# Layer-1 accumulators of a graph network kernel take seven PSUM banks in turn instead of five fixed ones, and the collect of a head is issued after the second multiply of the next head, not the third

## The reference

```python
def gat_conv(x, src, dst, W, a_src, a_dst, bias, H, C, n):
    h = (x @ W).reshape(n, H, C)
    s_src = (h * a_src).sum(-1)
    s_dst = (h * a_dst).sum(-1)
    e = jax.nn.leaky_relu(s_src[src] + s_dst[dst], NEG_SLOPE)
    emax = jax.ops.segment_max(e, dst, num_segments=n)
    ee = jnp.exp(e - emax[dst])
    denom = jax.ops.segment_sum(ee, dst, num_segments=n)
    alpha = ee / denom[dst]
    out = jax.ops.segment_sum(alpha[:, :, None] * h[src], dst, num_segments=n)
    return out.reshape(n, H * C) + bias
...
x_norm = layer_norm(x, norm_g, norm_b)
out1 = gat_conv(x_norm, src, dst, W1, a_src1, a_dst1, b1, H1, C1, N)
out2 = gat_conv(out1, src, dst, W2, a_src2, a_dst2, b2, H2, C2, N)
combined = jnp.concatenate([x, out2], axis=-1)
return combined @ Wu + bu
```

## Time and profile before

| | |
|---|---|
| median of 3 runs | 898.29 us (898.15 to 898.86) |
| the profiled execution: its time, its span | 898.75 us, 897.0 us |
| busy: PE, DVE, ACT | 809.6, 611.8, 292.7 us |
| weight loads (PEld), beside the matmuls | 666.6 us |
| mean granted clock of TensorE | 0.96 of full speed |
| matmuls of the layer-1 heads (`ps<-g,att`) | 800 records, 136.4 us |

### The profile page before, as it was taken

One profiled execution on the slowest core, in us unless ns is written; L12 is line 12 of the kernel. 1 busy time (PEld: TensorE's weight loads), 2 busy tenths in 40 slices (PEclk: granted clock), 3 DMA queues, 4 the chain that ended last, 5 costly groups with the idle time before them and its releaser, 6 DMA issues.

```text
span 897.0 us, 12506 instructions
## 1 busy us (share of the span) xinstructions
PE 809.6 (90%) x4306; PEld 666.6 (74%) x4307; DVE 611.8 (68%) x1304; ACT 292.7 (33%) x530; POOL 18.2 (2%) x32
## 2 busy tenths in 40 slices
PE   4999999998988599999987787799998999999997
PEld 3856666564534398999965687578887888999997
DVE  1776666789999599999779899765641832212444
ACT  4425455363333543443322444322221411111000
POOL 3100000000000030000000000000000000000000
PEclk9999999999999789999997797799999999999999
DMA  8300000000000140110000300000003000000111
GB/s 291 133 1 1 1 0 0 1 1 1 1 0 0 21 158 1 60 60 1 1 1 0 132 1 1 2 1 1 1 1 124 1 1 1 1 1 1 53 70 50
DMA packets 9578, 26.39 MB, mean 29 GB/s; under 512 B 623, under 2 KB 2477, under 8 KB 9138
## 3 DMA queue, kind: packets, MB, share of 16 engines
q1 hardware_dynamic: 9522, 25.65, 8.5%
HBM read 21.78 MB, written 3.87 MB: 29 GB/s over the span
## 4 chain that ended last, share of the span: by engine, by line
PE 63%; DVE 25%; issue 5%; DVEq 3%; ACT 2%; DMA 1%; SPq 0%; ACTq 0%
PE ps L1093 60%; DVE scrap L514 7%; DVE att L676 6%; DVE att L640 5%; DVEq L322 1%; DMA w<-in_L_gnn_W 1%; DVE xohd L528 1%; DVE ohs_abc L525 1%; DVE h2x L663 1%; DVEq L525 1%; PE ps L1177 1%; DVE out L663 1%; DVE gw1lo L716 1%; ACT att L980 1%; PE ps L1209 1%
## 5 line engine op out<-in xcount | busy, mean ns | idle before, releaser
L1093 PE MATMUL ps<-g,att 128*128 128x193 f32 x800 | 136.4, 332 | 8.4 <-DVE att L640 5.8
L1093 PEld LDWEIGHTS ps<-g,att 128*128 128x128 f32 x800 | 132.4, 193 | 12.4 <-issue 6.2
L980 ACT ACTIVATE att<-att,ssrc 128x1250 f32<-128x1250 f32 x60 | 80.2, 1338 | 105.9 <-DVE att L676 105.8
L676 DVE SCALAR_TENSOR_TENSOR att<-uB,s 128x1250 f32<-128x1250 f32 x60 | 91.3, 1525 | 2.8 <-PE ps L1093 2.6
L640 DVE SCALAR_TENSOR_TENSOR att<-att,ct 128x1250 f32<-128x1250 f32 x60 | 88.1, 1469 | 4.0 <-ACT att L980 3.7
L1093 PE MATMUL ps<-wux,xT 128*128 128x384 f32 x240 | 83.8, 502 | 0.3
L1093 PE MATMUL ps<-wp,xT 128*128 128x388 f32 x240 | 83.2, 496 | 0.0
L1093 PE MATMUL ps<-yhi,ctr 128*128 128x384 f32 x200 | 67.7, 338 | 0.0
L1093 PEld LDWEIGHTS ps<-wux,xT 128*128 128x128 f32 x240 | 45.6, 196 | 29.4 <-issue 2.1
L1093 PEld LDWEIGHTS ps<-wp,xT 128*128 128x128 f32 x240 | 44.0, 190 | 28.2
L740 DVE SCALAR_TENSOR_TENSOR ylo_a<-ps,dinv,yhi 128x384 fp32r<-128x384 f32 x32 | 19.0, 616 | 62.6 <-ACT yhi L829 62.6
(11 more groups left out here) (236 smaller groups left out, 1417.7 us busy)
## 6 DMA issues: line engine op xcount, KB each, us to landing
wux<-in_L_gnn_Wu SPq DMA_DIRECT2D x2, 2304.0 KB, 15.6
gw<-in_L_gnn_W SPq DMA_DIRECT2D x2, 2304.0 KB, 10.2
uB<-u_dram SPq DMA_DIRECT2D x3, 1280.0 KB, 5.9
xs<-in_x SPq DMA_DIRECT2D x1, 3456.0 KB
out<-ybuf SPq DMA_DIRECT2D x9, 384.0 KB, 2.4
w<-in_L_gnn_W SPq DMA_DIRECT2D x1, 2304.0 KB, 8.7
w2x<-in_L_gnn_W SPq DMA_DIRECT2D x1, 576.0 KB, 9.7
wuo<-in_L_gnn_Wu SPq DMA_DIRECT2D x1, 576.0 KB
```

The costliest lines, as they stand in the source:

```text
L676: v.scalar_tensor_tensor(att[:, n % NA, 0:N], uB[:, hp % 2, 1, 0:N], s08[:, h, q:q + 1], uB[:, hp % 2, 0, 0:N], ALU.add, ALU.max).then_inc ...
L980: a.activation(at_, at_, ACT.Exp, bias=ssrc[:, h, q:q + 1]).then_inc(att_exp, 1)
L1093: return t.matmul(o, lhsT, rhs, start=start, stop=stop, **kw)
```

## The change

Accumulator b of layer-1 head hp now lies in the bank at place (5 hp + b) mod 7 of the list 0, 1, 2, 3, 4, 6, 7. Its first matmul waits for the accumulator seven places back, so accumulators 0 and 1 of a head no longer wait for the head just before, and 2, 3 and 4 wait for that head's 0, 1 and 2. Layer 2 keeps its banks and waits. The collect is issued after mult(1) of the next head instead of mult(2), in both layers.

```diff
+        def acc_bank(hp, b):
+            return (0, 1, 2, 3, 4, 6, 7)[(5 * hp + b) % 7] if hp < H1 else b
...
-                    acc = ps[:, b, 0:2 * wid].rearrange("p (t n) -> p t n", t=2)
+                    acc = ps[:, acc_bank(hp, b), 0:2 * wid].rearrange("p (t n) -> p t n", t=2)
...
-                    if q == 3 and before is not None:
+                    if q == 2 and before is not None:
                         collect(before)
...
-                        if q == 0 and half == 0 and hp > 0:
+                        if q == 0 and half == 0 and hp >= H1:
                             t.wait_ge(acc_out, 5 * (hp - 1) + b + 1)
+                        elif q == 0 and half == 0 and 5 * hp + b >= 7:
+                            t.wait_ge(acc_out, 5 * hp + b - 6)
...
-                        last = mm(ps[:, b, half * wid:(half + 1) * wid], att[:, n % NA, dt_ * P:(dt_ + 1) * P], rhs,
+                        last = mm(ps[:, acc_bank(hp, b), half * wid:(half + 1) * wid], att[:, n % NA, dt_ * P:(dt_ + 1) * P], rhs,
```

## The result

The changed kernel takes 893.62 us (median of 6, 891.60 to 893.98), the kernel before 898.55 us (median of 6, 897.93 to 900.07). The ratio is 0.994, with a 95% interval of 0.9927 to 0.9953: faster by 4.9 us, 0.6%. The profiled execution took 893.35 us, with a span of 891.6 against 897.0. Two launches further down took 964.76 and 1172.56 us at a mean granted clock of 0.82 and 0.65, and no median here counts them.

A forecast was written before the change was run, and what follows sets the result against it. The prediction took TensorE's layer-1 matmuls, with waits for VectorE's collect at three head boundaries, as the bound. Removing 5.49 us there, with nothing gained or lost elsewhere, gave 892.8 us against the median, range 890.6 to 894.9.

The forecast's parts named there:

- The waits for banks: Three layer-1 head boundaries: TensorE's waits for the collect cost 2.24, 1.63 and 1.62 us, 5.49 us in all, all recoverable.
- the lockstep with the collect: First tile of a following head: TensorE held to VectorE's 0.853 us per accumulator against its own 0.654, costing 0.80 us.
- No wait stays: Head 1's accumulators 2, 3, 4: banks out at 349.1, 350.0, 350.8 us, wanted at 351.9, 352.6, 353.2.
- VectorE's cover: Layer 1, mult(12) ends before TensorE asks for tile 12: 1.9 us to spare in head 1, then 1.4 and 0.9.
- The DMA: Head 2's `uB` lands at 368.4 us, its reader stands at 373.84: over 4 us of cover, nothing to pay.
- the end of layer 1: TensorE's last matmul of head 3 ends at 449.07 instead of 454.57 us, 5.50 earlier, and all that follows moves with it.
- Layer 2, zero: Collect of head 4 moves 2.80 us earlier, TensorE regains 2.8 of 7.44 us, but VectorE is the bound: value zero.
- The clock: Layer 1: granted clock stays 1.00 by the profile, sum unchanged; by the skill's rule it falls, 899.8 us, chance 0.03.
- The sum: Whole kernel: profiled 898.75 less 5.5 is 893.25 us; against the median 892.8 us, 0.61% faster.
- The second case of the forecast: After layer 2: full gain, but low-clock stretches fall on other instructions, costing or giving 1.3 us: 891.5 or 894.1; chance 0.20.

The follow-up runs named there:

- The runs with more work: Changed kernel with one or three more pre, writing the same values, in each of heads 1 and 2: 895.54 and 902.99 us.
- the controls of the changed one: Changed kernel with one more bounding instruction on VectorE and TensorE after each load of a window's range of edge chunks: 894.58 and 894.92 us.

## Why the prediction was right

The forecast was 892.8 us, in a range of 890.6 to 894.9; measured were 893.62. Against the median of before in the same comparison the gain is 4.9 us, forecast were 5.5.

- *The waits for banks, 5.49 us.* Measured 5.57 on the heads stretch, 5.70 from the first matmul. The two parts, the wait at the head and the lockstep with the collect, are both gone. The prediction called the second part hidden and took it from the period of a head and VectorE's pace. It was in the same table as the first, in the row of weight loads shown above: 2.6 us, beside 2.6 us of the matmuls' own waits.
- *"No wait stays", and VectorE's cover.* Right. 1.9, 1.4 and 0.9 us were worked out, 1.7, 1.6 and 1.8 measured, since VectorE no longer waits for the ring and loses less. mult(12), mult(22) and mult(32) start at 354.80, 387.79 and 420.27 us, 32.99 and 32.48 apart and not 33.26; the shorter period is the one into head 3, which has no `give_u`. The runs with more work show that the cover is real and small.
- *The DMA and the end of layer 1.* No wait of VectorE for `uB` appears, and the next stage starts 1.85 us behind its collect as before.
- *Layer 2, zero.* Right: 64.62 or 64.63 us in every run with the collect at either place. TensorE did get 2.8 us of its wait back, but only 0.7 us of that reached the end of head 5.
- *The clock.* The granted clock is 1.00 from 325.1 to 451.6 us in the changed kernel (a row of its stretches, columns as above):

```profile
325.10:451.60 126.50, 124.69 (x765) 124.19 (x762) 118.31 (x139) 47.31 (x38) 8.05 (x5) 1.00 0.09 32
```

By the rule of the Trainium skill that was weighed there (TensorE: Matmul & The Clock Gate, section "A second HAM failure mode: psum-queue depth-cycling"), the rotation should have cost it; the trace disagrees: it shows 1.00 with seven banks in turn. That page tells of a bf16 kernel with 512 columns, and here the matmuls are fp32 with 193. The clock fell between the third tile of head 0 and the end of head 3 only in the run with the collect at q = 4, behind a wait of 2.54 us, with the same seven banks.

What was off is the size of the rest. The sum took the stages outside the heads to move by nothing. They moved by +0.91, -0.13, -0.41 and -0.19 us between the two profiled executions, and that much comes and goes by itself: two traces of one and the same kernel, the controls of the changed one, differ by 1.45 us in the start (317.50 and 316.05), by 0.78 in the first two tiles (8.84 and 9.62) and by 0.58 between the layers (52.88 and 53.46). The second case of the forecast looked for such a shift, of 1.3 us, but behind layer 2, where it was 0.19; the largest piece stands ahead of the first head, where the change does nothing and no case looked. The difference between 5.5 and 4.9 us is within the interval of the ratio (892.0 to 894.3 us).

What the prediction did not see is that the change is two edits for one wait. It reasoned them together, though its own numbers would have parted them. With fixed banks head 1 wants accumulator b free at 350.63 + 0.654 b; a collect that starts at 348.2 gives it back at about 349.3 + 0.853 b (by the earlier trace rows TensorE starts 1.1 us behind the collect, so this is 0.2 later than the prediction's 349.1): 352.7 us against 353.2 for the last one, so never late. The wait is gone with the earlier collect alone (126.48 us). With the rotation alone 4.0 of the 5.6 us are had (128.02 us against 132.05), or 4.8 of 5.7 from the first matmul. Beside the earlier collect the rotation is only cover for a VectorE that is late, 1.05 us in the run where 1.55 us were put into each of two heads.

## What to carry to other kernels

Take the period of the loop and subtract the bound engine's own work: here that gave 5.5 us where the matmuls' row of the table of waits showed 2.6, because a lockstep of two engines leaves the matmuls' row busy. Then read the row of the weight loads as well: it held the other 2.6. When an evacuation is issued in a program order by hand, its place has a window: too late and the next accumulation waits for it, too early and the engine stands in front of it with the next producer queued behind. Here one tile earlier than the best place cost 4.9 us and two tiles later 13.8. Look for the cheap edit first: moving one call did by itself what two more banks were also meant to do. And a ring of buffers ties an instruction to the other engine's progress: what stands behind it in the queue cannot come earlier, however fast its engine is.

## What the runs showed of the hardware

- The granted clock of a stage differs between executions of the same kernel, and the stage's length with it: the first two tiles of head 0 took 8.84 us at a granted clock of 0.74 and 9.62 us at 0.68 in the two controls of the changed kernel (8.10 us at 0.81 in the run with the rotation alone). The stretch between the layers took 52.77 to 53.46 us in twelve traces and 54.62 and 55.04 in the two with the collect at q = 1 and with three extra pre; over these two stretches the granted clock was 0.79, against 0.81 and 0.82 in the two controls and 0.82 before. In the first of them it was 0.52 from 458 to 461 us, right behind head 3. Both traces are of the slowest execution of their kernel (901.12 us with a median of 898.71, 903.73 with 902.99), so this need not be the kernel's doing. What decides it was not settled.
- A wait of 2.54 us inside dense matmuls was followed by about 4 us near the lower level, at each of three boundaries, and cost 1.4 to 2.0 us beside itself. Waits of 1.29, 1.38 and 1.83 us were not. But a wait of 3.47 us, in the run with three extra pre, was not either: the granted clock stayed at 1.00 from 401 to 414 us. Ahead of head 5, a wait of 4.64 us was followed by 0.50 over 6 us, and a longer one, 7.44 us, by 0.60. So the length of the wait alone does not decide.
- The bank that a layer-1 matmul writes makes no difference: ten tiles take 32.67 us with banks 0 to 4 (the run with the earlier collect alone) and with seven in turn, while VectorE reads another bank.
